# A two-layer decoder on one core: attention prepared during a recurrence, and the recurrent bias moved into PSUM

## The reference

```
x += mamba(x)                                   # first layer
x += cross attention of x on ctx (ReLU q, k, v)
x += self attention (RMSNorm, after a LayerNorm)
x += 8 experts, 2 chosen per row, and a shared one
# second layer
n = layernorm(x)                                # per row
h_t = tanh(n_t @ Wi.T + bi + h_(t-1) @ Wh.T + bh)   # t = 0..127, all 32 sequences at once
x += h
n = layernorm(x)
x += (gated mix of attention on n and attention on ctx, q/k/v with biases) @ Wo + bo
x += 8 experts, 2 chosen per row
```

## Time and profile before

| | us |
|---|---|
| median of 3 runs | 3362.09 |
| the profiled execution | 3390.08 |
| its span, first to last instruction | 3387.8 |
| mean granted TensorE clock, share of 2.4 GHz | 0.926 |

### The profile page before, as it was taken

The page is one execution under the profiler, slowest core; times in us unless marked ns, Lnnn a source line. Parts: engine busy times, 40 slices in busy tenths (PEclk is TensorE's granted clock), DMA queues, the critical chain, the costliest instruction groups (busy, mean ns, idle before and its releaser), DMA issues.

```text
span 3387.8 us, 49137 instructions
## 1 busy us (share of the span) xinstructions
PE 2774.7 (82%) x16644; PEld 1896.4 (56%) x16644; DVE 1931.8 (57%) x3400; ACT 1531.5 (45%) x2627; POOL 1459.2 (43%) x1508
## 2 busy tenths in 40 slices
PE   6878778865887688877999999699488888866998
PEld 2333323323555366633788885498355555545887
DVE  3788887783887488851122223401489888871111
ACT  4655555543776466520122221343366666641222
POOL 3666666663454477626000004400155556542444
PEclk8988989997999799988999999799799999977999
DMA  9600000000003000012566662100100011005775
GB/s 326 200 1 0 0 1 0 1 0 25 18 13 128 13 1 0 1 53 82 168 196 190 196 195 86 46 1 1 34 14 27 27 36 34 24 26 155 205 219 147
DMA packets 135983, 244.90 MB, mean 72 GB/s; under 512 B 16144, under 2 KB 107792, under 8 KB 125328
## 3 DMA queue, kind: packets, MB, share of 16 engines
q1 hardware_dynamic: 115344, 208.33, 19.0%
q0 software_dynamic: 20448, 34.11, 4.1%
HBM read 154.17 MB, written 90.05 MB: 72 GB/s over the span
## 4 chain that ended last, share of the span: by engine, by line
PE 34%; POOL 6%; issue 6%; DVE 6%; ACT 3%; another core or an unknown queue 1%; POOLq 1%; DMA 1%; SPq 0%; DVEq 0%; ACTq 0%
PE PS L2127 9%; PE PS L2085 5%; PE PS L1742 4%; PE PS L2372 4%; PE PS L2360 4%; POOL e_hs L1338 2%; PE PS L1193 1%; POOL rows_in_place L784 1%; POOL e_qs L1341 1%; DVE e_mx L1241 1%; PE PS L1138 1%; PE PS L1733 1%; POOL rows_by_expert L2016 1%; ACT e_pr L1305 1%
## 5 line engine op out<-in xcount | busy, mean ns | idle before, releaser
L506 POOL TENSOR_TENSOR u_in<-dtx,b_rep 128x512 f32<-128x512 f32 x256 | 339.0, 1345 | 210.5 <-ACT b_rep L487 198.4
L479 PE MATMUL PS<-scaled,ident 128*128 128x512 f32 x512 | 309.8, 690 | 71.9 <-DVE scaled L516 71.1
L522 DVE TENSOR_TENSOR_SCAN state<-PS,u_in 128x512 f32<-128x512 f32 x256 | 312.7, 1222 | 94.6 <-ACT PS L495 24.4
L2148 ACT ACTIVATE d_act_b<-PS 128x256 f32<-128x256 f32 (+1 forms) x188 | 78.7, 420 | 509.4 <-PE PS L2127 440.8
L2127 PE MATMUL PS<-d_unit_T,d_w 128*128 128x256 f32 x1248 | 284.0, 381 | 1.0 <-ACT d_unit_T L2137 1.0
L2160 DVE TENSOR_TENSOR d_hid<-d_act_b,PS 128x256 f32<-128x256 f32 (+1 forms) x188 | 87.4, 466 | 323.1 <-ACT d_act_b L2148 304.9
L495 ACT ACTIVATE PS<-dt,decay_rate 128x508 f32<-128x508 f32 x256 | 174.2, 685 | 186.7 <-DVE state L522 185.8
L1338 POOL TENSOR_TENSOR e_hs<-e_pr 128x512 f32<-128x512 f32 x128 | 162.9, 1273 | 221.6 <-ACT e_pr L1305 219.1
L2127 PEld LDWEIGHTS PS<-d_unit_T,d_w 128*128 128x128 f32 x1248 | 235.2, 191 | 32.0 <-issue 1.4
L2421 POOL DMA_INDIRECT out<-f_y,f_token x78 | 121.2, 1553 | 189.0 <-DVE f_token L2405 128.9
L2085 PE MATMUL PS<-d_w,d_hid 128*128 128x256 f32 x880 | 198.2, 380 | 1.5 <-DVE d_hid L2160 1.5
(11 more groups left out here) (424 smaller groups left out, 6386.7 us busy)
## 6 DMA issues: line engine op xcount, KB each, us to landing
d_w<-in_d_w SPq DMA_DIRECT2D x41, 1024.0 KB, 5.0
f_w<-in_f_w SPq DMA_DIRECT2D x39, 1024.0 KB, 5.0
rows_in_place<-blank SPq DMA_DIRECT2D x136, 272.0 KB, 4.2
d_w<-in_d_w SPq DMA_DIRECT2D x41, 512.0 KB
f_unit_rows<-rows_in_place SPq DMA_DIRECT2D x39, 272.0 KB, 4.9
rows_by_expert<-zeros SPq DMA_DIRECT2D x39, 256.0 KB, 2.8
d_unit_rows<-rows_by_expert SPq DMA_DIRECT2D x39, 256.0 KB, 4.0
out_by_expert<-d_y_rows SPq DMA_DIRECT2D x39, 256.0 KB, 4.1
```

What stands on the lines that cost most here:

```text
L479: nc.tensor.matmul(YB[:, c], ident[:], scaled[:, (KD * n + c) % RC], start=False, stop=n == NS - 1).then_inc(m_y, 1)
L506: nc.gpsimd.tensor_tensor(u_in[:, k % RU], dtx[:, p, c], b_rep[:, n % RB], ALU.mult).then_inc(m_u, 1)
L522: nc.vector.tensor_tensor_scan(state[:, k % 2], DECAY[:, k % RD], u_in[:, k % RU], 0.0, ALU.mult, ALU.add).then_inc(m_h, 1)
```

## The change

1. The recurrence adds its bias by PE. The sum of both biases is turned once to two rows, `r_bias_T` (2 x 128). Of each pair of input products (k = 0 and 1) the first is preceded by a product of `r_bias_T` with a column of the identity, repeated over 128 columns, which writes the bias of half m into all of them. The tanh takes no bias operand.
2. `recurrence` is now made inside attention "e", after that stage's weights, vectors, context tile, `va` and router tiles are laid out, so that these don't overlap with the recurrence's tiles. SP issues e's loads, ScalarE takes the two gate tanhs, VectorE scales `e_wv` and builds the folded bias, and GpSimd clears `f_ones`, `f_run`, `f_rows` and `e_va`, all in the recurrence stage, behind each engine's front and ahead of its part in the 128 steps.
3. The adds of h to X move into stage e: PE turns groups 0 and 1 first, and a further group behind each of the front's parts 1 to 6 of group 0; VectorE adds group 0, takes its statistics, adds group 1, takes its statistics, and adds the other twelve pairs. The small products that need e's setup use PSUM bank 5 instead of 7 and open the stage on PE.
4. All three attention stages get the new order of `run`. In b and c VectorE does the statistics of groups 0 and 1 first and only then waits for the loads, makes `parity`, and clears `va` and the PSUM bank; ScalarE waits for `ones_set` behind the normalised rows of group 0; PE waits for the loads only at the first q product.

```diff
-        def setup_vector(dve):
-            nc.vector.memset(ones[:], 1.0)
+        def setup_pool(pool):
+            nc.gpsimd.memset(ones[:], 1.0)
             for e in range(E):
-                nc.vector.memset(run[:, e:e + 1], float(e * REGION // 128))
-            nc.vector.memset(rows[:], 0.0).then_inc(made, 1)
-
-        def setup_tensor(pe):
+                nc.gpsimd.memset(run[:, e:e + 1], float(e * REGION // 128))
+            nc.gpsimd.memset(rows[:], 0.0).then_inc(made, 1)
...
+        cT = t("cT", [128, 2, KD, GT]) if "ctx" in sets else None
+        va = t("va", [128, 2, A, GS, NH, 2 * DH])
+        st, mvs, rs = t("st", [128, GS, 6]), t("mvs", [128, GS, 2]), t("rs", [128, 8, GS])
+        spare, spare2 = t("spare", [128, 1]), t("spare2", [128, 1])
+        full, empty, back_in = s("full"), s("empty"), s("back_in")
+        FB = PS[:, 7]
+        SB = PS[:, 5]
+        router = early_router("f", mem, table, FB, SB, lambda *x: fb_number[x], full, empty, back_in, ROUTE) if table else None
+        inner = ahead() if ahead else None
...
-            nc.vector.memset(PS[:, 6], 0.0)
             nc.vector.tensor_reduce(parity[:], v["mask"].rearrange("p (r e) -> p e r", e=2), AX.X, ALU.add).then_inc(parity_set, 1)
             if biased:
                 dve.wait_ge(parity_set, 1)
                 for a in range(A):
                     for e in range(2):
                         nc.vector.tensor_scalar(bk_par[:, a, :, e], v[f"bk{a}"][:], parity[:, e:e + 1], None, ALU.mult)
-            if table:
-                router["setup_vector"](dve)
-            nc.vector.memset(va[:], 0.0).then_inc(ones_set, 1)
...
+            else:
+                nc.vector.memset(va[:], 0.0).then_inc(ones_set, 1)
+
+        def setup_pool(pool):
+            router["setup_pool"](pool)
+            nc.gpsimd.memset(va[:], 0.0).then_inc(ones_set, 1)
...
+        def constants_vector(dve):
+            nc.vector.memset(PS[:, 6], 0.0)
+            if table:
+                router["constants_vector"](dve)
+            if biased:
                 dve.wait_ge(x_done, 1)
-                if table:
-                    router["constants_vector"](dve)
-                nc.vector.tensor_tensor(v["bo"][:], v["bo"][:], FB[:, 0:D], ALU.add).then_inc(ready, 1)
+                nc.vector.tensor_tensor(v["bo"][:], v["bo"][:], SB[:, 0:D], ALU.add).then_inc(ready, 1)
...
+        def constants_tensor(pe):
+            if table:
+                router["constants_tensor"](pe)
             if biased:
                 pe.wait_ge(ready, READY_WIDE)
-                if table:
-                    router["setup_tensor"](pe)
                 for c in range(KD):
-                    step = nc.tensor.matmul(FB[:, 0:D], bv_wide[:, c], halves["wo"][:, c], start=c == 0, stop=c == KD - 1)
+                    step = nc.tensor.matmul(SB[:, 0:D], bv_wide[:, c], halves["wo"][:, c], start=c == 0, stop=c == KD - 1)
                 step.then_inc(x_done, 1)
-                pe.wait_ge(ready, READY_WIDE + 1)
...
+            if ahead:
+                dve.wait_ge(h_added, 2 * g + 2)
...
+                    if is_first(g) and part == ("q", 0):
+                        pe.wait_ge(loaded, 16 * n_loads)
+                        if biased:
+                            pe.wait_ge(ready, READY_WIDE)
...
+                if ahead and is_first(g) and 1 <= j < NG - 1:
+                    inner["add_tensor"](pe, j + 1, h_turned, h_added)
...
+            first()
             alone(early(eng, 0, 0))
+            second()
             alone(front(eng, 0, 0))
             alone(early(eng, 1, 1))
+            third()
...
+            def consts_taken():
+                pe.wait_ge(ones_set, 1)
+                if biased:
+                    pe.wait_ge(ready, READY_WIDE + 1)
+
+            constants_tensor(pe)
+            if ahead:
+                inner["add_tensor"](pe, 0, h_turned, h_added)
+                inner["add_tensor"](pe, 1, h_turned, h_added)
+            run(pe, none, front_tensor, units_tensor, back_tensor, 0, third=consts_taken)
...
+            def after_setup():
+                act.wait_ge(parity_set, 1)
+                act.wait_ge(ones_set, 1)
+
+            run(act, early_scalar, front_scalar, units_scalar, none, 2, second=after_setup)
 
         def vector(dve):
-            setup_vector(dve)
-            run(dve, early_vector, none, units_vector, back_vector, 1)
+            def add(lo, hi):
+                for g in range(lo, hi if ahead else lo):
+                    inner["add_vector"](dve, g, h_turned, h_added)
+
+            def rest():
+                add(2, NG)
+                if not ahead:
+                    setup_vector(dve)
+                constants_vector(dve)
+
+            run(dve, early_vector, none, units_vector, back_vector, 1, first=lambda: add(0, 1), second=lambda: add(1, 2), third=rest)
...
+            sp.wait_ge(cleared, following["cleared"])
+            following["sync"](sp)
...
+            dve.wait_ge(bias_in_T, 1)
+            nc.vector.tensor_copy(bias_T[:], PS[0:KD, 0, 0:128]).then_inc(bias_set, 1)
...
+            pe.wait_ge(bias_set, 1)
+            nc.tensor.transpose(PS[0:KD, 0, 0:128], bias[:], ident[:]).then_inc(bias_in_T, 1)
+            pe.wait_ge(bias_set, 2)
...
-                nc.tensor.matmul(window(w, odd, m)[:, 0], wi_k[:, k, m * 128:m * 128 + 128], xT_w[:, k, w, :, odd],
-                                 start=k == 0, stop=k == KD - 1)
+                z = window(w, odd, m)[:, 0]
+                if k == 0:
+                    nc.tensor.matmul(z, bias_T[:], ident[0:KD, m:m + 1].unsqueeze(2).broadcast_to([KD, Q, B]), start=True, stop=False)
+                nc.tensor.matmul(z, wi_k[:, k, m * 128:m * 128 + 128], xT_w[:, k, w, :, odd], start=False, stop=k == KD - 1)
...
-            pe.wait_ge(copied, 2 * TURNS + 1)
-            for b in range(B):
+        def add_tensor(pe, g, turned, added):
+            for b in range(GS * g, GS * g + GS):
                 if b % 2 == 0 and b >= 4:
                     pe.wait_ge(added, b // 2 - 1)
                 for c in range(KD):
-                    step = nc.tensor.transpose(PS[:, 4 + b // 2 % 2, (b % 2 * KD + c) * 128:(b % 2 * KD + c) * 128 + 128], HS[:, c, b], ident[:])
+                    step = nc.tensor.transpose(PS[:, 3 + b // 2 % 2, (b % 2 * KD + c) * 128:(b % 2 * KD + c) * 128 + 128], HS[:, c, b], ident[:])
                 if b % 2:
                     step.then_inc(turned, 1)
 
+        def add_vector(dve, g, turned, added):
+            x_seq = X.rearrange("p g s d -> p (g s) d")
+            for b in range(GS * g, GS * g + GS, 2):
+                dve.wait_ge(turned, b // 2 + 1)
+                nc.vector.tensor_tensor(x_seq[:, b:b + 2], x_seq[:, b:b + 2],
+                                        PS[:, 3 + b // 2 % 2].rearrange("p (b d) -> p b d", b=2), ALU.add).then_inc(added, 1)
...
+            act.wait_ge(cleared, following["cleared"])
+            following["scalar"](act)
             act.wait_ge(copied, 1)
-            act.wait_ge(bias_set, 1)
 
             for at in range(L):
                 if at % WIN == 0:
                     after(act, copied, at // WIN)
                 for m in range(KD):
                     act.wait_ge(ready[m], at + 1)
-                    nc.scalar.activation(ring[:, m, at % (2 * WIN)], bank(at, m)[:, 0], ACT.Tanh, bias=bias[:, m:m + 1]).then_inc(tanhed[m], 1)
+                    nc.scalar.activation(ring[:, m, at % (2 * WIN)], bank(at, m)[:, 0], ACT.Tanh).then_inc(tanhed[m], 1)
...
+            dve.wait_ge(cleared, following["cleared"])
+            following["vector"](dve)
...
+            following["pool"](pl)
```

More of the change, by code:

```diff
@@ L1419, in attention, with nothing, run @@
         s_x1c = s("x1c")
-        def run(eng, early, front, units, back, n=None):
+        def nothing():
+            return
+        def run(eng, early, front, units, back, n=None, first=nothing, second=nothing, third=nothing):
             def turn(g, p):
@@ L1618, in feature_rows, with recurrence @@
         return dict(vector=vector, pool=pool, scalar=scalar, tensor=tensor, kept=kept)
[L1624 removed]
+    def recurrence(tag, turn, following):
         WIN = 8
```

74 lines of the change are left out of this document (31 added, 43 removed).

## The result

Measured: 3330.28 us, the median of 4 runs (3329.13 to 3338.53), against 3361.65 for the kernel before in the same session. The ratio is 0.9913, with a 95% interval of 0.9895 to 0.9930. The kernel is faster by 31 us. The forecast was 3309.6 with a range of 3297 to 3327: the sign was right, the size was not, and the time lies outside the range.

The account below looks back on a forecast made before the run. The recurrence was taken as a PE, ACT, PE latency loop, and starts of e, b and c as waiting on setup. Gains 3.5 (recurrence) + 32.2 (e) + 16.8 (b, c) = 52.5 us, from 3362.1 to 3309.6; range 3297 to 3327.

Parts of the forecast that it names:

- the price of the two-row product: Recurrence: the added bias product costs 0.22 us of PE, so steps carrying one are PE-bound at 1.335 us.
- the 0.43 of the low clock: Recurrence: upper end for the two-row product, a product's price at the low clock, 0.43 us.
- Rival B: Recurrence: tanh not shorter, total 3315, or two-row product dearer, at 0.43 us 3322; chance 0.10.
- The start of the recurrence: Ahead of step 0: four two-row products join the first window's eight input products, +0.9 us.
- The tanh fell by 0.09 us: Recurrence: tanh without bias operand 0.09 us shorter, so a step without a two-row product can fall to 1.22.
- 4.4 less: Recurrence steps: 59 x 0.02 more, 68 x 0.09 less and 0.5 for handing on, together -4.4 us.
- The start of e: Stage e, last `r_HS` copy to first scores: 70.6 us falls to 38.4, a gain of 32.2 us.
- rival D: Front of stage e: adds don't lie beside it, six groups each wait 1.44 us, total 3318; chance 0.08.
- b and c: Starts of attention stages b and c: first copies come 7.4 and 9.4 us earlier, together 16.8 us.
- The clock stayed full: Recurrence: PE's clock expected to stay full; a rival had it lost, up to 3447 us, chance 0.02.
- the 28: Profiled execution before lay 28 us above the median of the runs, place unknown; the prediction carried this over unscaled.
- several times that: GpSimd's clearings beside the recurrence: may cost several times VectorE's time, but were costed at nothing given 222 us idle.

Follow-up runs that it names:

- grouped run: Changed kernel with the four two-row bias products of a window issued together in the window's first step: 3316.09 us, ratio 0.9858.
- 128-row kernel: Changed kernel with the recurrence's bias product made of 128 rows instead of two, rows 2 to 127 zero: 3306.31 us, ratio 0.9837.
- 96- and 128-row runs: Changed kernel with the bias product padded by zero rows to 96 or 128 rows instead of two: 3306.23 and 3306.31 us.

## Why the prediction was wrong, point by point

**The step that failed** is the price of the two-row product: "I take the full-clock price of any product with 128 columns, 0.22". The product itself has that price (0.22 a product in the grouped run, 0.22 with 96 and 128 rows), but between full ones it brings two changes of the number of rows, at each of which the next load no longer runs beside the product before it: 0.40 us together. The steps that carry one take 1.725 us, where I had 1.335 and the 128-row kernel has 1.34. The recurrence of the changed kernel exceeds that kernel's by 26.2 us (190.8 and 164.6): 58 steps by 0.385 are 22.3, and the first four steps, two of them with a product, take 9.2 instead of 5.3, which is the other 3.9. They are slow above all because TensorE ran them at the low level: its granted clock is 0.50 until 2151, 7 us behind the first product of step 0 (2143.82), and in the 128-row kernel it is 0.71 in the microsecond from 2145 and 1.00 from 2146 on, 1 us behind that product (2144.96). Against the forecast the recurrence missed by 25.4. Every upper end that I wrote down, the 0.43 of the low clock among them, was a price of an instruction; none was a price of a switch between kinds of instructions, so the bounds had no place for it. Rival B at 0.43 gives a step of 0.21 more and 3322, still 8 us short. The warning was in the trace of before, which mixes products of 32 and of 128 rows in stage e: I read from it only the time of the eight 32-row ones, not the time between the two kinds. These are PE's loads there, behind eight transposes of 128 rows each (the clock is 1.00 at both places):

```profile
2450.97 0.91 PEld L1193 LDWEIGHTS PS<-ident,e_pr 128*128 128x128 f32 x8
2451.85 0.30 PEld L1138 LDWEIGHTS PS<-e_xT,e_wq 128*128 128x128 f32 x2
...
2572.80 0.91 PEld L1193 LDWEIGHTS PS<-ident,e_pr 128*128 128x128 f32 x8
2573.87 0.31 PEld L1184 LDWEIGHTS PS<-e_kT,e_q 32*128 32x128 f32 x8 [0.17 <-issue]
```

Eight loads at 0.11 are 0.89. Another 128-row load follows at 0.88, the 32-row load at 1.07, with no wait that the profile names: 0.2 later, the price of one change as in the recurrence.

**The neighbouring rule.** The rule of the Trainium skill that I weighed (page "TensorE: Matmul & The Clock Gate", Why this matters for your kernels) says that a lone product of few rows takes as long as a full one. The grouped run agrees (0.11 a pair, as for 128 rows). It was not the rule that decides here.

**The start of the recurrence** was +3.7 instead of +0.9. The 0.9 for four more products is confirmed (31.9 to 32.8). Turning the bias, which I put beside ScalarE's last copy, adds 0.7 (32.8 to 33.5). The other 2.1 (33.5 to 35.6) go with the row count alone, as the 96- and 128-row runs show: the breaks once more, at the low clock. A two-row product with its two input products takes 1.87 us there (loads at 2138.34 and 2140.21), with 128 rows 1.28 (2140.91 and 2142.19), so a break costs 0.30, and seven of them lie ahead of step 0.

**What was right.** The tanh fell by 0.09 us and the steps without a two-row product to 1.22. With 96 or 128 rows the recurrence takes 164.6, 5.2 less than before, where the prediction had 4.4 less; and those kernels' 3306 us are within 4 us of the forecast. The start of e gave 33.8 of the predicted 32.2 us: 3.3 to the first statistics (predicted 3.6), then 33.5 (predicted 34.8). That rules out rival D. b and c gave 17.2 of 16.8. The clock stayed full once it had risen, 7 us into the recurrence. The chance of 0.97 for faster rested on these terms and held; the range failed because it was bounded below the one unknown price.

**Checked against the sum.** -33.8 for e, -17.2 for b and c, +21.0 and +3.7 for the recurrence make -26.3. The medians differ by 31.4. Of the remaining 5 us the two profiles show 2.0 ahead of stage b, 1.1 in b and c (they differ by 18.3 there), 1.4 between c and the recurrence beyond the 28, and 1.0 behind the first scores of e. The profiles don't say why; it is of the size of what single executions scatter.

## What to carry to other kernels

A product over few rows is not free next to full ones: in this stream of 128-row fp32 products, one of 2, 32 or 64 rows cost 0.40 us beyond its own 0.22, and zero rows up to 96 or 128 took that away. Pad small products until they no longer break the stream (96 rows did here), or group them, or give the work to an engine that idles: VectorE's addition in place did it within 0.7 us of no bias at all. When an unknown instruction is bounded, bound the transitions around it too, from the starts of the neighbouring loads and not only from mean durations.

## What the runs showed of the hardware that was not expected

The change of the number of rows: 0.20 us each way at the full clock and 0.30 at the low one, for 2, 32 and 64 rows against 128, none for 96. The 32-row scores of the attention stages pay it too behind 128-row transposes, as the loads of stage e above show. What it would save to pad or regroup them was not tried.

The clock rose late where the breaks were. Its granted share reached 1.00 within 1 us of the first product of step 0 with 96 or 128 rows, and only 7 us behind it with 2 or 32 (4 with 64), though PE was busy throughout by the profile. Why, no run here shows.

VectorE's small instructions stretched beside a clearing on GpSimd. In the timeline of after:

```profile
2132.97 6.93 POOL L1001 MEMSET e_va<- 128x8192 f32 x1
...
2136.01 3.94 DVE L975 TENSOR_SCALAR e_bk_par<-e_bk,e_parity 128x2 f32<-128x2 f32 x4
2136.53 3.44 DVE L978 TENSOR_SCALAR e_share<-e_share 128x16 f32<-128x16 f32 x1
...
2140.02 0.17 DVE L981 TENSOR_SCALAR e_share<-e_share 128x16 f32<-128x16 f32 x1
```

The clearing ends at 2139.90, and the instructions of lines 975 and 978 end within 0.08 us of it, the first of line 978 in 3.44 us where the next of its kind and size takes 0.17. The copy and the reduction just before, also beside the clearing, took 0.28 and 0.16, so not every VectorE instruction is held. The Trainium skill has the rule, on its page "SBUF — State Buffer" (SBUF: two separate sides): VectorE in its two-port mode and GpSimd share a pair of ports, and whichever comes first has it for its whole instruction. The trace agrees for the held instructions. That the mode is what tells them from the two that passed, no run here shows. Here nothing waited for them. The clearing itself was as fast on GpSimd as it had been on VectorE: 6.93 against 6.89 us for 128x8192, where I had feared several times that.
